# A fused cross-attention and feed-forward block: another order for the first units, feed-forward factors in five portions, and the value factor ahead of the third chunk's rows

## The chip, the cores and the metric

The kernel runs on one core of a Trainium2 chip. The metric is the device time of one execution in microseconds (us); lower is better. A core has four compute engines with queues of their own, TensorE (PE, matmuls), VectorE (DVE), ScalarE (ACT) and GpSimd (POOL), and SyncE (SP), which here issues nearly all DMAs. Each engine takes its instructions in the order of its own program; between engines there are only semaphores, waited for by hand.

## The reference, cut to what matters

```python
def reference(x, ctx, mask, g_xattn, g_ffn, ...):      # x (2, 2048, 512), ctx (2, 128, 512)
    # cross-attention, 16 heads of 32; x normalised twice, ctx once
    q = (layer_norm(_layernorm(x), g_x, b_x) @ w_q)     # 2048 queries a batch
    k, v = layer_norm(ctx, g_kv, b_kv) @ w_kv           # 128 keys a batch
    attn = softmax(where(mask == 0, -1e9, q @ k.T * SCALE))
    x = x + tanh(g_xattn[0]) * ((attn @ v) @ w_proj + b_proj)
    # feed-forward, 512 -> 2048 -> 512, weights (q - 128) * scale by groups of 128 rows
    h = layer_norm(_layernorm(x), ln_gamma, ln_beta)
    z = silu(h @ w1 + fc1_bias) @ w2 + fc2_bias
    return x + tanh(g_ffn[0]) * (_layernorm(x) + 0.5 * z)
```

(`_layernorm` is without gain and shift; the residual of the feed-forward part is its own normalised input.)

## The kernel before

All large products are made of parts: each operand is split into a high and a low part, and three matmuls (high x high, high x low, low x high) stand for one product (`split_product`).

**Attention.** The 4096 rows are 8 chunks of 512; a chunk has 4 blocks of 128 columns, that is 4 heads each. One chunk and one block make a *unit*, v = 0 to 31. Every engine has its own `step(i, k)`, and `every_step` runs it for v = 8i + k: steps -8 to 7 written out (i = 0), two rounds of a loop of 8 steps, and the last steps written out. A dictionary gives work that is put ahead of a given step (`setup`). `real(i, k, n)` tells whether the unit exists. What belongs to one unit is spread over many steps. TensorE in step k does, in this order:

- `scores_for_max(k+1)` on token tiles 0 and 1: unmasked scores, whose maximum over the keys VectorE takes (`take_max`); `ps_max` has two banks, so tile t waits for the maximum of tile t-2, and tile 1 also for `max_row` of the unit before, whose turned maxima lie in the same bank;
- the first half of `queries(k+2)`, six matmuls; then tiles 2 and 3 of `scores_for_max(k+1)`; then the second half of `queries(k+2)`, six matmuls;
- `turn_x(k+6)`: four transposes of the normalised x;
- `weighted_values(k-1)`: probabilities times values, and the sums of the probabilities; its last matmul raises `pv_done`;
- `turn_maxima(k+1)`: the maxima turned into rows;
- `scores(k, j)` for heads j = 0, 1, then (from step 5 on with halves of `project(k-5)` between) 2 and 3. There are two banks `ps_s`, so scores j wait for the exponentials of scores j-2. Scores 0 also wait for the packed queries and packed maxima, which come by DMA (`q_packed`, `max_packed`).

ScalarE in step k: `take_queries(k+2)` (`q_hi`), `take_x(k+6)` (`xt_hi`, `xt_f`), `take_maxima(k+1)` (`max_row`), then for each of four heads `p_f` and `p_hi` (`probabilities`), then `outputs_hi(k-1)` (`o_hi`). In `probabilities`:

```python
after(act, s_done, HG * v + j + 1)
after(act, *lo_taken(i, k - 1, j))
nc.scalar.activation(p_f[j][:, :], ps_s[j % 2][:, :], ACT.Exp, ...)
after(act, pv_done, v)          # weighted_values of unit v - 1 has read the old p_hi
nc.scalar.activation(p_hi[j][:, :], ps_s[j % 2][:, :], ACT.Exp, ...)
```

VectorE in step k: the maxima of unit k+1 (tiles 0, 1), `add_residual(k-6)`, maxima of tiles 2, 3, `rows_in_step(k, 0)`, `queries_lo(k+2)` (`q_lo`, waits for `q_hi`), `rows_in_step(k, 1)`, `invert_sums(k-1)` (`den_t`, `inv_t`, `inv_den`; waits for `pv_done`), `p_lo` of heads 0 and 1, `normalise(k-1)` (`o_f`). `rows_in_step` spreads the layer norm of later chunks: statistics (`row_stats`) in steps with k mod 4 = 3, `normalise_rows` in the two steps behind them; the factors between (`row_scales`, seven small operations) are GpSimd's. Chunk 2 is the third; it has its statistics in step -1 and its normalisation in steps 0 and 1.

GpSimd in step k: `xt_lo` of block k+6, the bias on the residual, `row_scales`, `p_lo` of heads 2 and 3, `o_lo(k-1)`.

SyncE in step k: `pack_queries(k+1)` (three DMAs of 256 KB, `q_dram` to `q_pack`), loads of x, residual loads and stores of the result, `store_queries(k+2)` (`q_hi`, `q_lo` to memory), `pack_maxima(k+1)` (four DMAs of 2 KB, `max_row` to `q_pack`, L491).

**Setup around the first steps.** Ahead of VectorE's step 0 stands `value_parts`: from the bound of the values it makes the scale `v_scale`, then the low part of the values (the high part is ScalarE's, `values_first_part`), and copies the four largest magnitudes `most`. Ahead of its step 6 stands `ffn_numbers`: 13 small operations that make the scales of the feed-forward part (`ffn_scales`).

**Feed-forward.** 128 steps of 24 matmuls of 512 columns, in which TensorE hardly ever waits.

Of the kernel before, what the change touches and what calls it, by code (L numbers as in the profile page):

```python
# [37 lines left out]
HG = P // HEAD  # L38
# [3 lines left out]
V_RANGE = 16384.0  # L42
W_RANGE = 0.125
H_RANGE = 356.0
Y_RANGE = 32768.0
Y_BOUND = 131072.0
# [197 lines left out]
def attention(nc, env):  # L244
# [33 lines left out]
    with ExitStack() as scope:  # L278
# [121 lines left out]
        def normal_rows(i, c):  # L400

            return x_rows(c) if real(i, KB * c, UNITS) else x_norm

        def in_tail(i, k):

            return isinstance(i, int) and PER * i + k >= UNITS - 3
# [140 lines left out]
        def _(pe):  # L547
# [96 lines left out]
            def step(i, k):  # L644
# [7 lines left out]
                if real(i, k + 1, UNITS):  # L652
                    scores_for_max(i, k + 1, (2, 3))
                if real(i, k + 2, UNITS):
                    queries(i, k + 2, second)
# [4 lines left out]
                if real(i, k + 1, UNITS):  # L660
                    turn_maxima(i, k + 1)
                if real(i, k, UNITS):
                    scores(i, k, 0)
                    scores(i, k, 1)
# [80 lines left out]
        def _(act):  # L745
# [44 lines left out]

            def step(i, k):
                if real(i, k + 2, UNITS):
                    take_queries(i, k + 2)
                if real(i, k + AHEAD, UNITS + KB):
                    take_x(i, k + AHEAD)
                if real(i, k + 1, UNITS):
                    take_maxima(i, k + 1)
                if real(i, k, UNITS):
                    for j in range(HG):
                        probabilities(i, k, j)  # L800
                if real(i, k - 1, UNITS):
                    outputs_hi(i, k - 1)
                if isinstance(i, int):
                    last_steps(PER * i + k)
# [59 lines left out]
        def _(dve):  # L864
# [78 lines left out]
            def rows_in_step(i, k, half):  # L943

                c = k // KB + 2
                spread = not isinstance(i, int) or 2 * i + c >= 2 and real(i, KB * c, UNITS)
                if k % KB == 3 and (not isinstance(i, int) or 2 * i + c + 1 >= 2):
                    row_stats(i, c + 1, range(TT // 2 * half, TT // 2 * (half + 1)))
# [7 lines left out]
            def step(i, k):  # L956
# [9 lines left out]
                if real(i, k + 2, UNITS):  # L966
                    queries_lo(i, k + 2)
                rows_in_step(i, k, 1)
                if real(i, k - 1, UNITS):
# [63 lines left out]

            def ffn_numbers():

# [4 lines left out]
                nc.vector.tensor_scalar(w2_scale, inv_most[:, 2:3], W_RANGE, None, ALU.mult)  # L1040
                nc.vector.tensor_scalar(h_gain, lng_c, inv_most[:, 0:1], H_RANGE, ALU.mult, ALU.mult)
                nc.vector.tensor_scalar(h_shift, lnb_c, inv_most[:, 0:1], H_RANGE, ALU.mult, ALU.mult)
                link(nc.vector.tensor_tensor(y_unscale, most[:, 0:1], most[:, 1:2], ALU.mult))
                link(nc.vector.scalar_tensor_tensor(out=y_bound, in0=y_unscale, scalar=Y_BOUND, in1=most[:, 3:4],
                                                    op0=ALU.mult, op1=ALU.add))
                link(nc.vector.tensor_scalar(y_unscale, y_unscale, 1.0 / (W_RANGE * H_RANGE), None, ALU.mult))
                link(nc.vector.reciprocal(y_scale, y_bound))
                link(nc.vector.tensor_scalar(y_scale, y_scale, Y_RANGE, None, ALU.mult))
                link(nc.vector.tensor_tensor(z_unscale, y_bound, most[:, 2:3], ALU.mult))
                dve.wait_ge(tanh_ready, 2)  # L1050
                nc.vector.tensor_scalar(z_unscale, z_unscale, half_gate[:, :], 1.0 / (W_RANGE * Y_RANGE),
                                        ALU.mult, ALU.mult).then_inc(scales_ready, 1)

# [37 lines left out]

            def value_parts():

                dve.wait_ge(v_summed, 1)
                link(nc.vector.reciprocal(v_bound[:, :], ps_s[0][:, 0:1]))
                link(nc.vector.tensor_scalar(scale16[:, :], all_ones[:, 0:HEAD], v_bound[:, :], V_RANGE, ALU.mult, ALU.mult))
                nc.vector.tensor_copy(v_scale[:, :], scale16[:, 0:1]).then_inc(v_scaled, 1)
                dve.wait_ge(v_scaled, 1)
                for b in range(B):
# [3 lines left out]
                last.then_inc(v_ready, 1)  # L1103
                dve.wait_ge(most_spread, 1)
                nc.vector.tensor_copy(most, ps_s[1][:, 0:4]).then_inc(most_ready, 1)
                nc.vector.memset(pause[:, :], 0.0).then_inc(setup_over, 1)

            def last_steps(u):

                if u in (UNITS + 1, UNITS + 3):  # L1110
# [3 lines left out]
            every_step(dve, step, {-8: context_rows, -7: lambda: [masks(), scale_maxima()], -4: lambda: [key_parts(), row_stats(0, 1), key_means()], -1: lambda: [value_bound(), scale_maximum()],  # L1114
                              0: value_parts, 6: ffn_numbers})

        @block.gpsimd
        def _(pool):
# [64 lines left out]
            def step(i, k):  # L1183
# [4 lines left out]
                if k == FIRST:  # L1188
                    row_scales(i, 0)
                if k % KB == 3 and (not isinstance(i, int) or 2 * i + k // KB + 3 >= 2):  # L1190
                    row_scales(i, k // KB + 3)
# [3 lines left out]
                if real(i, k - 1, UNITS):  # L1195
                    outputs_lo(i, k - 1)
                if isinstance(i, int) and PER * i + k == UNITS:
                    sum_scales()
# [372 lines left out]
```

## Time and profile before

| what | value |
|---|---|
| median of 3 runs | 1101.06 us (1099.99 to 1102.05) |
| the profiled execution, its own time | 1101.9 us |
| its span, first to last instruction | 1100.1 us |
| mean granted TensorE clock | 0.981 of full |
| TensorE busy | 1034.4 us, 94% |
| VectorE, ScalarE, GpSimd busy | 648.1, 399.2, 328.7 us |
| attention steps 0 to 7 | 52.3 to 147.3 us |
| feed-forward part | from about 415 us to the end |

The profiled execution's time is 0.8 us above the median, its span 1.0 below it. Engines overlap, so busy times don't add up; what matters is where TensorE stands still.

### The profile page before, as it was taken

The numbers are of one execution on the slowest core, as the hardware profiler recorded it, in microseconds if no ns is written. First come the engines' busy times: TensorE is split into PE (matmuls) and PEld (weight loads), VectorE is DVE, ScalarE is ACT, GpSimd is POOL, SyncE is SP. The second block draws the span as 40 slices with busy tenths as digits, with TensorE's granted clock in tenths as the row PEclk, the third lists the DMA queues.
The fourth block names the chain that finished last, engine by engine and source line by source line (L and its number), as shares of the span: only waits on it lengthen the run. The fifth ranks groups of instructions, "written<-read, shape, count | busy, mean of one in ns | idle before, by whom it ended". The sixth has DMA issues, their size and how long they took to land.

```text
span 1100.1 us, 15132 instructions
## 1 busy us (share of the span) xinstructions
PE 1034.4 (94%) x5182; PEld 564.0 (51%) x5182; DVE 648.1 (59%) x1070; ACT 399.2 (36%) x612; POOL 328.7 (30%) x338
## 2 busy tenths in 40 slices
PE   5777899999999878999999999999999999999998
PEld 3444567767766553444444444444444444444443
DVE  5667798898888757786335335346345335335322
ACT  3457577777776633331121121121121121121111
POOL 4545477677675442202102102102102012012000
PEclk9889899999999989999999999999999999999999
DMA  8566567778666669602001001100100200200101
GB/s 275 134 163 175 163 192 212 213 201 238 194 196 179 188 185 278 239 1 77 1 1 49 28 1 39 39 1 28 51 1 1 77 1 1 77 1 1 39 1 39
DMA packets 61473, 109.38 MB, mean 99 GB/s; under 512 B 9656, under 2 KB 10848, under 8 KB 60896
## 3 DMA queue, kind: packets, MB, share of 16 engines
q1 hardware_dynamic: 58632, 104.11, 31.2%
q10 hardware_dynamic: 2776, 4.40, 1.4%
q8 instruction: 41, 0.67, 0.3%
q14 instruction: 24, 0.20, 0.1%
HBM read 72.57 MB, written 33.55 MB: 96 GB/s over the span
## 4 chain that ended last, share of the span: by engine, by line
PE 57%; DVE 3%; issue 1%; ACT 1%; DVEq 0%
PE ps_z L1387 9%; PE ps_z L1389 9%; PE ps_z L1388 9%; PE ps_y L238 9%; PE ps_y L240 9%; PE ps_y L239 9%; PE ps_h L1401 1%; DVE w_f L192 1%; ACT w_hi L183 1%; DVE w_lo L195 0%; DVE y_hi L1448 0%; DVE x_in L1509 0%; DVE x_stats L1489 0%; DVE x L1471 0%; DVE x_norm L1501 0%
## 5 line engine op out<-in xcount | busy, mean ns | idle before, releaser
L1422 ACT ACTIVATE y_f<-ps_y,cols,ffn_scales 128x512 f32<-128x512 f32 x128 | 99.4, 777 | 489.5 <-PE ps_y L240 489.5
L1448 DVE TENSOR_SCALAR y_hi<-y_f,ffn_scales 128x512 f16<-128x512 f32 x128 | 70.0, 547 | 330.4 <-ACT y_f L1422 330.4
L1387 PE MATMUL ps_z<-w_hi,y_hi 128*128 128x512 f16 x512 | 194.7, 380 | 3.6 <-DVE w_lo L195 3.6
L238 PE MATMUL ps_y<-ht_hi,w_hi 128*128 128x512 f16 x512 | 194.1, 379 | 1.6 <-PEq L278 1.5
L1388 PE MATMUL ps_z<-w_lo,y_hi 128*128 128x512 f16 x512 | 194.6, 380 | 0.0
L1389 PE MATMUL ps_z<-w_hi,y_lo 128*128 128x512 f16 x512 | 194.6, 380 | 0.0
L239 PE MATMUL ps_y<-ht_lo,w_hi 128*128 128x512 f16 x512 | 194.0, 379 | 0.0
L240 PE MATMUL ps_y<-ht_hi,w_lo 128*128 128x512 f16 x512 | 194.0, 379 | 0.0
L1450 DVE SCALAR_TENSOR_TENSOR y_lo<-y_f,ffn_scales,y_hi 128x512 f16<-128x512 f32 x128 | 103.2, 806 | 4.6
L761 ACT ACTIVATE p_f<-ps_s,fill_col 128x512 f32<-128x512 f32 x128 | 86.2, 673 | 3.5 <-PE ps_s L592 3.5
L763 ACT ACTIVATE p_hi<-ps_s,fill_col 128x512 f16<-128x512 f32 x128 | 85.3, 666 | 0.0
L870 DVE TENSOR_REDUCE maxima<-ps_max 128x4 f32<-128x512 f32 x128 | 81.9, 680 | 5.6 <-PE ps_max L569 5.3
L238 PEld LDWEIGHTS ps_y<-ht_hi,w_hi 128*128 128x128 f16 x512 | 50.1, 98 | 62.6 <-issue 2.5
L1152 POOL TENSOR_TENSOR p_lo<-p_f,p_hi 128x512 f16<-128x512 f32 x58 | 67.8, 1175 | 47.9 <-ACT p_hi L763 47.5
L1387 PEld LDWEIGHTS ps_z<-w_hi,y_hi 128*128 128x128 f16 x512 | 50.2, 98 | 61.3 <-DVE w_lo L195 4.1
L1389 PEld LDWEIGHTS ps_z<-w_hi,y_lo 128*128 128x128 f16 x512 | 50.2, 98 | 60.9 <-issue 0.8
L240 PEld LDWEIGHTS ps_y<-ht_hi,w_lo 128*128 128x128 f16 x512 | 50.1, 98 | 60.4
L239 PEld LDWEIGHTS ps_y<-ht_lo,w_hi 128*128 128x128 f16 x512 | 50.1, 98 | 60.2
L1388 PEld LDWEIGHTS ps_z<-w_lo,y_hi 128*128 128x128 f16 x512 | 50.2, 98 | 57.6 <-issue 0.6
L1527 POOL TENSOR_TENSOR ln_a<-x_mean_var,eps 128x4 f32<-128x4 f32 x7 | 1.6, 224 | 254.9 <-DVE x_mean_var L1494 254.9
L1545 POOL TENSOR_TENSOR x<-x,b_rows 128x512 f32<-128x512 f32 x16 | 25.8, 1645 | 141.5 <-DVE x L1509 141.5
L907 DVE TENSOR_TENSOR p_lo<-p_f,p_hi 128x512 f16<-128x512 f32 x70 | 53.6, 783 | 19.3 <-ACT p_hi L763 18.6
(200 smaller groups left out, 1585.9 us busy)
## 6 DMA issues: line engine op xcount, KB each, us to landing
q_pack<-q_dram SPq DMA_DIRECT2D x96, 256.0 KB, 4.0
q_dram<-q_hi SPq DMA_DIRECT2D x32, 256.0 KB, 3.2
q_dram<-q_lo SPq DMA_DIRECT2D x32, 256.0 KB, 3.6
x_dram<-x_out SPq DMA_DIRECT2D x32, 256.0 KB, 4.6
x_res<-in_x SPq DMA_DIRECT2D x30, 256.0 KB, 4.5
q_raw<-in_L_ffn_fc_q SPq DMA_DIRECT2D x6, 1024.0 KB, 8.8
s_raw<-in_L_ffn_fc_scales SPq DMA_DIRECT2D x6, 1024.0 KB, 11.8
x_in<-in_x SPq DMA_DIRECT2D x4, 1024.0 KB, 7.8
```

Of the source, the lines that this page charges most:

```text
L238: nc.tensor.matmul(out, s_hi, m_hi, start=(k == 0), stop=False)
L239: nc.tensor.matmul(out, s_hi, m_lo, start=False, stop=False)
L240: last = nc.tensor.matmul(out, s_lo, m_hi, start=False, stop=(k == n - 1))
L761: nc.scalar.activation(p_f[j][:, :], ps_s[j % 2][:, :], ACT.Exp, bias=fill_col[:, b:b + 1]).then_inc(p_f_ready, 1)
L763: nc.scalar.activation(p_hi[j][:, :], ps_s[j % 2][:, :], ACT.Exp, bias=fill_col[:, b:b + 1]).then_inc(p_hi_ready, 1)
L870: nc.vector.reduce_max(maxima[k % 2][:, t, :], ps_max[t % 2][:, :].rearrange("p (j n) -> p j n", j=HG), AX.X).then_inc(max_taken, 1)
L1387: nc.tensor.matmul(ps_z[t][:, :], hi, w2_hi[:, f, :], start=(f == 0), stop=False)
L1388: nc.tensor.matmul(ps_z[t][:, :], hi, w2_lo[:, f, :], start=False, stop=False)
L1389: last = nc.tensor.matmul(ps_z[t][:, :], lo, w2_hi[:, f, :], start=False, stop=(f == FB - 1))
L1422: nc.scalar.activation(y_f[f % 2][:, :], ps_y[f % 2][:, :], ACT.Silu, bias=b1_c[:, f:f + 1], scale=y_unscale).then_inc(y_f_ready, 1)
L1448: nc.vector.tensor_scalar(y_hi[f % 4][:, :], y_f[f % 2][:, :], y_scale, None, ALU.mult).then_inc(y_hi_ready, 1)
L1450: nc.vector.scalar_tensor_tensor(out=y_lo[f % 4][:, :], in0=y_f[f % 2][:, :], scalar=y_scale, in1=y_hi[f % 4][:, :], op0=ALU.mult, op1=ALU ...
```

## The change

Three things are changed.

1. For units 1 to 4 (`unprojected`: the steps that have no projection yet) TensorE issues scores 0 and 1 ahead of the second half of `queries(k+2)`, instead of behind `turn_maxima`; ScalarE does the probabilities of heads 0 and 1 first in its step, ahead of `take_queries`.
2. `value_parts` is split: `value_scale` (the scale, and the copy of `most`) stays ahead of VectorE's step 0; the low part of the values (`value_rest`) goes into step 0, behind `queries_lo`. The statistics of chunk 2 go from step -1 to step 0, behind that, its row factors on GpSimd to the end of step 0, and the normalisation of all its four tiles to step 1, behind `queries_lo`.
3. `ffn_numbers` is split into `weight_scales`, `hidden_bound`, `hidden_scales`, `row_gain` and `row_shift`, ahead of VectorE's steps 2, 3, 4, 5 and 6. `hidden_bound` has one operation more (a lower bound on `y_bound`). The ranges to which weights and hidden values are scaled, immediates of operations that were there, go from 0.125 to 2^-8 and from 32768 to 256.

```diff
-W_RANGE = 0.125
+W_RANGE = 2.0 ** -8
-Y_RANGE = 32768.0
+Y_RANGE = 256.0
...
+        def unprojected(i, k):
+            return isinstance(i, int) and 1 <= PER * i + k < 5
...
     # TensorE, step
                 if real(i, k + 1, UNITS):
                     scores_for_max(i, k + 1, (2, 3))
+                if unprojected(i, k):
+                    scores(i, k, 0)
+                    scores(i, k, 1)
                 if real(i, k + 2, UNITS):
                     queries(i, k + 2, second)
...
-                if real(i, k, UNITS):
+                if real(i, k, UNITS) and not unprojected(i, k):
                     scores(i, k, 0)
                     scores(i, k, 1)
...
     # ScalarE, step
             def step(i, k):
+                if unprojected(i, k):
+                    probabilities(i, k, 0)
+                    probabilities(i, k, 1)
                 if real(i, k + 2, UNITS):
                     take_queries(i, k + 2)
...
-                    for j in range(HG):
+                    for j in range(HG // 2 if unprojected(i, k) else 0, HG):
                         probabilities(i, k, j)
...
     # VectorE, rows_in_step
-                if k % KB == 3 and (not isinstance(i, int) or 2 * i + c + 1 >= 2):
+                if isinstance(i, int) and PER * i + k in (0, 1):
+                    if half == 1:
+                        row_stats(0, 2) if k == 0 else normalise_rows(0, 2)
+                    return
+                if k % KB == 3 and (not isinstance(i, int) or 2 * i + c + 1 > 2):
...
     # VectorE, step
                 if real(i, k + 2, UNITS):
                     queries_lo(i, k + 2)
+                if isinstance(i, int) and PER * i + k == 0:
+                    value_rest()
                 rows_in_step(i, k, 1)
...
-            def ffn_numbers():
+            def weight_scales():
                 dve.wait_ge(most_ready, 1)
                 link(nc.vector.tensor_scalar(most, most, 1e-30, None, ALU.max))
                 link(nc.vector.reciprocal(inv_most[:, 0:3], most[:, 0:3]))
                 nc.vector.tensor_scalar(w1_scale, ...)
                 nc.vector.tensor_scalar(w2_scale, ...)
-                nc.vector.tensor_scalar(h_gain, lng_c, inv_most[:, 0:1], H_RANGE, ALU.mult, ALU.mult)
-                nc.vector.tensor_scalar(h_shift, lnb_c, inv_most[:, 0:1], H_RANGE, ALU.mult, ALU.mult)
                 link(nc.vector.tensor_tensor(y_unscale, most[:, 0:1], most[:, 1:2], ALU.mult))
+            def hidden_bound():
                 link(nc.vector.scalar_tensor_tensor(out=y_bound, ...))
                 link(nc.vector.tensor_scalar(y_unscale, ...))
+                link(nc.vector.tensor_scalar(y_bound, y_bound, 1e-30, None, ALU.max))
                 link(nc.vector.reciprocal(y_scale, y_bound))
+            def hidden_scales():
                 link(nc.vector.tensor_scalar(y_scale, ...))
                 link(nc.vector.tensor_tensor(z_unscale, ...))
                 dve.wait_ge(tanh_ready, 2)
                 nc.vector.tensor_scalar(z_unscale, ...)
+            def row_gain():
+                nc.vector.tensor_scalar(h_gain, lng_c, inv_most[:, 0:1], H_RANGE, ALU.mult, ALU.mult)
+            def row_shift():
+                nc.vector.tensor_scalar(h_shift, ...).then_inc(scales_ready, 1)
...
-            def value_parts():
+            def value_scale():
                 ...
                 nc.vector.tensor_copy(v_scale[:, :], scale16[:, 0:1]).then_inc(v_scaled, 1)
+                dve.wait_ge(most_spread, 1)
+                nc.vector.tensor_copy(most, ps_s[1][:, 0:4]).then_inc(most_ready, 1)
+            def value_rest():
                 dve.wait_ge(v_scaled, 1)
                 for b in range(B):
                     dve.wait_ge(v_first, b + 1)
                     last = nc.vector.scalar_tensor_tensor(out=v_parts[1][:, b, :], ...)
                 last.then_inc(v_ready, 1)
-                dve.wait_ge(most_spread, 1)
-                nc.vector.tensor_copy(most, ps_s[1][:, 0:4]).then_inc(most_ready, 1)
                 nc.vector.memset(pause[:, :], 0.0).then_inc(setup_over, 1)
...
-                              0: value_parts, 6: ffn_numbers})
+                              0: value_scale, 2: weight_scales, 3: hidden_bound, 4: hidden_scales, 5: row_gain, 6: row_shift})
...
     # GpSimd, step
-                if k % KB == 3 and (not isinstance(i, int) or 2 * i + k // KB + 3 >= 2):
+                if k % KB == 3 and (not isinstance(i, int) or 2 * i + k // KB + 3 > 2):
                     row_scales(i, k // KB + 3)
...
                     outputs_lo(i, k - 1)
+                if isinstance(i, int) and PER * i + k == 0:
+                    row_scales(0, 2)
```

## Rows read from the trace of the kernel before

**Rows 1.** The page, busy time, share of the span and instructions, TensorE.

```profile
PE 1034.4 (94%) x5182; PEld 564.0 (51%) x5182; DVE 648.1 (59%) x1070; ACT 399.2 (36%) x612; POOL 328.7 (30%) x338
```

**Rows 2.** Windows of steps 6 and 7: stretch, busy time per engine, clock, DMA.

```profile
120.72:137.61 16.89, 12.84 (x61) 8.53 (x60) 11.82 (x26) 7.75 (x14) 6.08 (x5) 0.80 0.58 171
137.61:147.30 9.69, 9.69 (x61) 7.02 (x60) 9.49 (x21) 7.56 (x14) 7.30 (x7) 1.00 0.62 193
```

**Rows 3.** Timeline, steps -1 and 0, VectorE and TensorE: start, duration, operation, wait.

```profile
52.60 1.29 DVE L923 BATCH_NORM_STATS2 x_stats<-x_in 128x6 f32<-128x512 f32 x2 [2.09 <-DMA x_in<-in_x]
...
59.77 1.00 PE L569 MATMUL ps_max<-k_hi,q_hi 128*128 128x512 f32 x2 [3.55 <-DVE maxima L870]
```

**Rows 4.** Timeline of TensorE, end of step 1 and the scores.

```profile
73.36 0.39 PE L240 MATMUL ps_qm<-xt_hi,wq_lo 128*128 128x512 f32 x1
73.59 0.60 PE L622 MATMUL ps_xp<-ident,x_norm 128*128 128x128 f32 x4
...
77.73 0.49 PE L592 MATMUL ps_s<-q_pack,k_pack 97*128 97x512 f32 x1 [1.35 <-ACT p_hi L763]
```

**Rows 5.** Timeline of ScalarE, step 1.

```profile
73.79 0.60 ACT L750 ACTIVATE q_hi<-ps_qm 128x512 fp32r<-128x512 f32 x1 [3.48 <-PE ps_qm L240]
...
75.95 0.58 ACT L782 CAST max_row<-ps_max 4x512 fp32r<-4x512 f32 x1 [0.22 <-PE ps_max L577]
76.43 0.67 ACT L761 ACTIVATE p_f<-ps_s,fill_col 128x512 f32<-128x512 f32 x1
77.01 0.66 ACT L763 ACTIVATE p_hi<-ps_s,fill_col 128x512 f16<-128x512 f32 x1
```

**Rows 6.** SyncE's queue, packed maxima: timeline; landing of 58.1 to 58.8, of 76.5 to 78.4.

```profile
56.39 2.95 SPq L491 DMA_DIRECT2D q_pack<-max_row  x4
...
86.14 3.70 SPq L491 DMA_DIRECT2D q_pack<-max_row  x4
...
DMA to landing us min/median/max: 2.8/2.9/3.0
...
DMA to landing us min/median/max: 1.7/1.7/1.7
```

**Rows 7.** Timeline of VectorE, steps 1 to 5.

```profile
75.48 0.71 DVE L886 STREAM_TRANSPOSE den_t<-ps_den 128x512 f32<-128x512 f32 x1
...
95.67 1.28 DVE L923 BATCH_NORM_STATS2 x_stats<-x_norm 128x6 f32<-128x512 f32 x2
...
97.38 0.68 DVE L886 STREAM_TRANSPOSE den_t<-ps_den 128x512 f32<-128x512 f32 x1
...
100.79 2.68 DVE L870 TENSOR_REDUCE maxima<-ps_max 128x4 f32<-128x512 f32 x4
104.67 0.69 DVE L877 SCALAR_TENSOR_TENSOR q_lo<-ps_qm,q_hi 128x512 fp32r<-128x512 f32 x1 [1.20 <-ACT q_hi L750]
105.28 1.00 DVE L940 TENSOR_SCALAR x_norm<-x_norm,x_mean_var,ln_r 128x512 f32<-128x512 f32 x2
106.19 0.71 DVE L886 STREAM_TRANSPOSE den_t<-ps_den 128x512 f32<-128x512 f32 x1
...
116.50 0.71 DVE L886 STREAM_TRANSPOSE den_t<-ps_den 128x512 f32<-128x512 f32 x1
```

**Rows 8.** Timeline of VectorE and TensorE, the feed-forward factors and behind them.

```profile
121.15 1.16 DVE L1037 TENSOR_SCALAR ffn_scales<-ffn_scales 128x4 f32<-128x4 f32 x1
...
123.42 1.31 DVE L1042 TENSOR_SCALAR ffn_scales<-cols,ffn_scales 128x4 f32<-128x4 f32 x1
...
126.75 1.30 PE L569 MATMUL ps_max<-k_hi,q_hi 128*128 128x512 f32 x2 [4.05 <-DVE maxima L870]
```

**Rows 9.** Timeline of GpSimd beside them.

```profile
123.44 1.26 POOL L1132 TENSOR_TENSOR o_lo<-o_f,o_hi 128x512 fp32r<-128x512 f32 x1
```

**Rows 10.** A window of 3.2 us behind the scores of step 3, columns as in rows 2.

```profile
88.40:91.60 3.20, 3.14 (x7) 2.48 (x8) 2.56 (x4) 2.80 (x6) 1.91 (x2) 0.50 0.26 55
```

More of the change, by code:

```diff
@@ L1050, in ffn_numbers @@
                 dve.wait_ge(tanh_ready, 2)
-                nc.vector.tensor_scalar(z_unscale, z_unscale, half_gate[:, :], 1.0 / (W_RANGE * Y_RANGE),
-                                        ALU.mult, ALU.mult).then_inc(scales_ready, 1)
+                nc.vector.tensor_scalar(z_unscale, z_unscale, half_gate[:, :], 1.0 / (W_RANGE * Y_RANGE), ALU.mult, ALU.mult)
+            def row_gain():
+                nc.vector.tensor_scalar(h_gain, lng_c, inv_most[:, 0:1], H_RANGE, ALU.mult, ALU.mult)
+            def row_shift():
+                nc.vector.tensor_scalar(h_shift, lnb_c, inv_most[:, 0:1], H_RANGE, ALU.mult, ALU.mult).then_inc(scales_ready, 1)
             def key_parts():
```

## The prediction

> **What bounds the kernel now.** I read the page first: TensorE is busy for 94% of the span [rows 1], so a change pays only where TensorE stands still or its clock is low. Then I cut the first 150 us into the kernel's own steps (one unit per step). From step 7 on a step takes 9.69 us, with TensorE busy in every one of them; step 6 takes 16.89 us, at a clock of 0.80 [rows 2]. Everything behind step 7 follows TensorE, so what the first steps win or lose should arrive at the end one to one. Last I read the timelines of each engine through steps 0 to 6, for which wait ends last there.
>
> I count from T(v), the moment at which `weighted_values` has finished unit v-1 in step v. VectorE's `den_t` starts at once behind it, so the trace has it: T(1) = 75.48, T(5) = 116.50, thus 41.0 us for four cycles [rows 7].
>
> Three losses are seen. In step 0 TensorE waits 3.55 us for VectorE's maxima, which stand behind the statistics of chunk 2 (these waited 2.09 us for their rows from memory) and the value factor [rows 3]. In each of steps 1 to 4 it waits 1.35 us ahead of score 2, for the exponential of head 0, and again, more shortly, ahead of score 3 [rows 4]. In step 6 it waits 4.05 us for maxima behind `ffn_numbers` [rows 8], and its matmuls are slow for a while after.
>
> **The change, part by part.**
>
> *Step 0.* With the statistics gone from step -1, `q_lo`(1), the value scale and the maxima of unit 1 come as soon as TensorE delivers them, and the 3.55 us wait goes. What is late next is the packed maximum of unit 0: SyncE issues its four small DMAs from 56.39, behind the query DMAs of its in-order queue, which the change leaves alone; the last is issued at 58.8 and lands 2.9 later [rows 6], so scores(0,0) come at 61.7, not at 64.3. The first exponential follows 0.5 later, the next three starts 0.57 apart and 0.66 for the last [rows 5]: score 3 at 64.6. Then, at 0.23 a matmul [rows 4], two scores for the maxima, six of queries, two, the two early scores of unit 1 and six more end at 69.0; turning x and the weighted values take 1.89 [rows 4, 7]: T(1) = 70.9, **4.6 us earlier**. The statistics of chunk 2 (2.4, plus 0.5 to join them) now lie behind the value factor, under the wait for those scores; GpSimd's row factors for them come behind its share of unit 0, near 68 to 71.5, before step 1's normalisation wants them.
>
> *The new order, steps 1 to 4.* TensorE now issues scores 0 and 1 of unit k ahead of the second half of queries(k+2), the turn of x and `weighted_values(k-1)`; ScalarE takes `p_f`, `p_hi` of both heads ahead of `take_queries(k+2)`. But `probabilities` waits for `pv_done` before it writes `p_hi`, and that is `weighted_values(k-1)`, which stands behind the early scores. So ScalarE starts `p_hi`(0) only at T, and queued behind it are everything that it did before T in the old order. From T, with the starts of [rows 5]: `p_hi`(0) at 0.05, `p_f`(1), `p_hi`(1), then `q_hi` at 1.76, done at 2.36; from its start to the end of the two copies of x it is 1.94 (73.79 to 75.95, less the wait of 0.22), so `max_row` runs from 3.70 to 4.28. Two chains leave here.
> VectorE has stood waiting in `queries_lo` since about T-2: `q_lo` from 2.40, `den_t` 0.61 on, from there 3.41 to the first maximum of unit k+2 (inversion, two `p_lo`, `o_f`), and 1.29 for two maxima [rows 7]: T+7.71. Only then may TensorE score tile 3, at +0.23 issue S0(k+1), S1, and with 0.23 x 6 of queries and 1.89 reach T(k+1) = T + 11.67.
> SyncE: `max_row` at 4.28, fourth DMA issued 1.8 later, landed 1.7 later [rows 6]: T+7.8. The two chains end together, so neither alone being shorter helps. The old waits ahead of scores 2 and 3 become one before tile 1 (for `max_row`, which lives in the same PSUM bank) and one before tile 2.
>
> *What VectorE gets on that chain.* Whatever stands between `q_lo` and the maxima lengthens a cycle in full. Cycle 1: all four tiles of chunk 2 normalised in one go, 1.8 (0.91 for two [rows 7]), and the first portion of the feed-forward factors, about 0.8. Cycle 2: four small dependent operations of 0.19, one of them new: 0.8. Cycle 3: the second half of the statistics of chunk 3, 1.7 [rows 7], and a portion of 0.5. Cycle 4: two tiles 0.9 and the row gain, 0.4. Sum 6.9. So 4 x 11.67 + 6.9 = 53.6 against 41.0: **12.6 us later**.
>
> *Step 6.* Of `ffn_numbers` (from 121.15; TensorE gets its maximum at 126.75) one operation is left ahead of the maxima. It is four columns wide, yet one such took 1.31 us and ended at 124.73, just as GpSimd's operation ended at 124.70 [rows 8, 9]. I give it 1.25, of which the step's slack takes 0.35, so 0.9 on TensorE; with the plain step of 9.7 to 9.8 [rows 2] that is 10.7 for 16.9: **6.2 us earlier**. Three of the old operations were of the long kind; spread out they cost 0.15 where GpSimd is idle, 1.2 where it is not. That is the bound of each portion; I take the short value except in steps 5 and 6.
> The Trainium skill ("SBUF — State Buffer", Who interferes with whom) says that VectorE and GpSimd share a pair of SBUF ports as an exclusive lock and that a tensor_scalar can take it; the ends in rows 8 and 9 agree. By that rule the normalisation of cycle 1, itself a tensor_scalar, could also stand behind GpSimd's `xt_lo` of 1.3 us, which would make the sum about 1.2 larger.
>
> *The clock.* TensorE runs at 1.2 instead of 2.4 GHz in some stretches after it stood still: 3.2 us at 0.50 from 88.40 [rows 10], the matmuls then 0.43 apart instead of 0.23. In steps 1 to 4 of the old trace this hit two of four cycles, about 1.2 us each. At the start the new kernel stands still from 58.0 to 61.7 and nearly so to 64.6, so I expect the 12 matmuls up to the early scores slow: 12 x 0.2 = **2.4 us later** (bounds 0 and 4.5). In the new cycles the critical TensorE work is the tail (six queries, turn, weighted values), worth 2.6 if all slow. TensorE is now idle some 5 us or more of 12 to 14. Bounds: nothing, and 4 x 2.6 = 10.4; I take two hits of half size beyond those already in the 41.0, **2.7 us later**.
>
> *No cost.* `W_RANGE` and `Y_RANGE` are immediates of operations that stay; feed-forward matmuls, weights and DMAs are the same instructions. SyncE's program is unchanged. `value_rest` ends near 60, ahead of the exponentials at 62.2, which cover it.
>
> Sum: -4.6 + 2.4 + 12.6 + 2.7 - 6.2 = +6.9 us. The profiled execution took 1101.9 (span 1100.1), 0.8 above the median of 1101.06. On the median: **1108.0 us**.
>
> **Rivals.**
> 1. *The clock stays up in the new cycles and at the start.* For it: of four gaps of one size in the old steps only two were followed by a slow stretch. Sum 1.8: 1102.9, no measurable change. This is also the case in which the three parts merely cancel. Against it: the gaps grow.
> 2. *Faster: the early exponentials do not lengthen the cycle.* If `weighted_values` were done by the time that ScalarE wants it, and VectorE's tail lay beside TensorE's work, four cycles stay at 41.0: -4.6 + 2.4 - 6.2 = -8.4, 1092.7. It decides below 47.2 us for the four (11.8 each), where the gain reaches 0.2%. Against it: my bare cycle alone is 11.67 and the known extras add 1.7 each.
> 3. *Packed maxima later.* At 86.14 the four issues took 3.70 instead of some 2.4 us [rows 6], just after a chunk of x was fetched, hidden there; in the new order it ends the chain. Twice 2 us: 1112.
> 4. *The port lock in cycle 1 and in the portions*: 1.2 more, 1109.2; no case of its own.
>
> **How the numbers follow.** Chances: forecast 0.60, rival 1 0.13, rival 2 0.14, rival 3 0.13. 0.2% (2.2 us) is what this kernel's times can tell from none. Slower 0.73, same 0.13, faster 0.14. The forecast's own range is 1104 to 1113 (cycle clock 0 to 7 us). The range reaches down into rival 2's slow half, 1098, and up to 1113; the all-slow bound (1117) is left out.
>
> **What the profile would show.** Right: scores(0,0) near 61.7; T(1) near 73; `q_hi` of steps 1 to 4 directly behind two or more exponentials that start at T; VectorE idle 4 us before each `q_lo` there; cycles of 12.5 to 16; no 4 us wait in step 6; T(5) near 130, T(6) near 140 and some 7 later than before (116.50 + 16.9). Wrong: `p_hi`(0) not waiting for T, or cycles near 10, would refute the main term; a T(1) near 75 the start; a step 6 above 12 the last.

## The result, and the profile after

The changed kernel takes **1118.86 us** (median of three, 1118.26 to 1120.33) against 1101.06: a ratio of 1.0167 [1.0148, 1.0186]. Slower, as forecast, but by 17.8 us and not 6.9, and outside the range of 1104 to 1113.

The page of the kernel after, busy time (share of the span) and instructions of each engine, against [rows 1]:

```profile
span 1117.0 us, 15131 instructions
PE 1043.5 (93%) x5182; PEld 567.3 (51%) x5182; DVE 651.2 (58%) x1071; ACT 399.3 (36%) x612; POOL 329.8 (30%) x338
```

VectorE has one instruction more and TensorE as many as before, with 9.1 us more of busy time for the same matmuls: part of them ran slower. To place the rest I use a mark that the prediction only wrote as T: `turn_maxima` starts on TensorE directly behind `weighted_values`. Its starts in steps 1 to 6, read off TensorE's timeline (`ps_max<-ident,maxima`), and what lies between:

| | step 1 | four cycles (1 to 5) | step 5 to 6 |
|---|---|---|---|
| before | 75.31 | 41.03 | 16.91 |
| after | 72.55 | 67.71 | 10.66 |
| difference | -2.76 | +26.68 | -6.25 |

The three differences make +17.7 at the end of step 6; the spans differ by 16.9, the medians by 17.8. So the whole loss lies in four cycles of one kind. These are marks of one execution of each kernel. A kernel below that shares all code with the kernel before up to step 1's mark reaches it at 76.83 instead of 75.31, so a difference of some 1.5 us or less between two traces is no proof of a cause. The windows of the kernel after, one cycle each and then step 6, and last a tail that is read further down. Columns: stretch, its length, busy time of TensorE, weight loads, VectorE, ScalarE, GpSimd, granted clock, DMA share, GB/s.

```profile
72.55:90.50 17.95, 11.11 (x53) 6.59 (x49) 10.93 (x20) 7.68 (x13) 5.08 (x4) 0.71 0.44 134
90.50:106.92 16.42, 11.60 (x53) 7.01 (x50) 9.97 (x17) 7.68 (x13) 5.31 (x4) 0.69 0.30 81
106.92:123.51 16.59, 10.97 (x52) 6.58 (x48) 8.52 (x21) 7.68 (x13) 8.52 (x11) 0.79 0.36 97
123.51:140.26 16.75, 10.43 (x50) 6.00 (x47) 11.03 (x17) 9.03 (x15) 5.52 (x5) 0.80 0.41 119
140.26:150.92 10.66, 10.29 (x64) 7.00 (x60) 8.42 (x13) 7.23 (x13) 5.88 (x5) 1.00 0.52 130
102.20:105.70 3.50, 3.50 (x11) 2.51 (x9) 1.38 (x3) 0.48 (x1) 0.00 (x0) 0.50 0.00 0
```

TensorE stands still for 4.8 to 6.8 us of each cycle, and the clock averages 0.69 to 0.80; in the old steps 6 and 7 it was 0.80 and 1.00 [rows 2]. No engine is busy for more than 11.6 of some 17 us: this is a chain of waits, not a busy engine. The second cycle, followed from T = 90.5, ScalarE's timeline of the kernel after (start, duration, operation, the wait ahead of it and what ended it):

```profile
90.62 0.69 ACT L770 ACTIVATE p_hi<-ps_s,fill_col 128x512 f16<-128x512 f32 x1 [3.77 <-PE ps_den L615]
91.20 0.68 ACT L768 ACTIVATE p_f<-ps_s,fill_col 128x512 f32<-128x512 f32 x1
91.77 0.69 ACT L770 ACTIVATE p_hi<-ps_s,fill_col 128x512 f16<-128x512 f32 x1
92.34 0.60 ACT L757 ACTIVATE q_hi<-ps_qm 128x512 fp32r<-128x512 f32 x1
...
94.14 0.56 ACT L789 CAST max_row<-ps_max 4x512 fp32r<-4x512 f32 x1
```

`p_hi`(0) waits 3.77 us for `ps_den`, the end of `weighted_values(1)`: the wait for `pv_done` that the prediction named (2.57, 4.36 and 4.72 in the other three). Three exponentials later comes `q_hi`, at T+1.84; `max_row` stands at T+3.64. Forecast were 1.76 and 3.70. VectorE's timeline of the same cycle, and two later lines:

```profile
92.98 0.69 DVE L887 SCALAR_TENSOR_TENSOR q_lo<-ps_qm,q_hi 128x512 fp32r<-128x512 f32 x1 [6.42 <-ACT q_hi L757]
93.59 0.70 DVE L896 STREAM_TRANSPOSE den_t<-ps_den 128x512 f32<-128x512 f32 x1
...
95.25 2.50 DVE L917 TENSOR_TENSOR p_lo<-p_f,p_hi 128x512 f16<-128x512 f32 x2
97.68 0.68 DVE L909 TENSOR_TENSOR o_f<-ps_o,inv_den 128x512 f32<-128x512 f32 x1
98.28 0.50 DVE L1060 SCALAR_TENSOR_TENSOR ffn_scales<-ffn_scales 128x1 f32<-128x1 f32 x1
...
99.39 1.29 DVE L880 TENSOR_REDUCE maxima<-ps_max 128x4 f32<-128x512 f32 x2
...
129.19 3.09 DVE L917 TENSOR_TENSOR p_lo<-p_f,p_hi 128x512 f16<-128x512 f32 x2
...
145.08 1.16 DVE L1076 TENSOR_SCALAR ffn_scales<-cols,ffn_scales 128x4 f32<-128x4 f32 x1
```

VectorE stands still for 6.42 us, since its queue is held at `q_lo`; `den_t`, which it could have done at T, comes 3.1 late. And TensorE, same kernel, same cycle, with the tail up to T = 106.9:

```profile
100.23 1.30 PE L573 MATMUL ps_max<-k_hi,q_hi 128*128 128x512 f32 x2 [2.55 <-DVE maxima L880]
101.33 1.06 PE L596 MATMUL ps_s<-q_pack,k_pack 97*128 97x512 f32 x2
102.18 0.63 PE L238 MATMUL ps_qm<-xt_hi,wq_hi 128*128 128x512 f32 x1
102.61 0.63 PE L239 MATMUL ps_qm<-xt_lo,wq_hi 128*128 128x512 f32 x1
...
104.74 1.06 PE L626 MATMUL ps_xp<-ident,x_in 128*128 128x128 f32 x4
```

The last wait to end ahead of the tail is for VectorE's maxima, not for a DMA. Then the matmuls start 0.43 apart instead of 0.23 [rows 4]: the last window above has the clock at 0.50 throughout.

### The profile page after: what moved, and what is told of

Read it like the earlier page. It is cut to its first block, busy times and chain, and to the rows that moved or that the text cites. A ratio compares the mean times of both kernels' runs of the same rounds, so it can differ in the third digit from the quotient of the medians.

```text
span 1117.0 us, 15131 instructions
## 1 busy us (share of the span) xinstructions
PE 1043.5 (93%) x5182; PEld 567.3 (51%) x5182; DVE 651.2 (58%) x1071; ACT 399.3 (36%) x612; POOL 329.8 (30%) x338
## 4 chain that ended last, share of the span: by engine, by line
PE 56%; DVE 3%; issue 1%; ACT 1%; DVEq 0%
PE ps_z L1418 9%; PE ps_z L1417 9%; PE ps_z L1416 9%; PE ps_y L240 9%; PE ps_y L238 9%; PE ps_y L239 9%; PE ps_h L1430 1%; DVE w_f L192 1%; ACT w_hi L183 1%; DVE w_lo L195 0%; DVE y_hi L1477 0%; DVE x_in L1538 0%; DVE x_stats L1518 0%; DVE x L1500 0%; DVE x_norm L1530 0%
## 5 line engine op out<-in xcount | busy, mean ns | idle before, releaser
L573 PE MATMUL ps_max<-k_hi,q_hi 128*128 128x512 f32 x128 | 46.8, 437 | 26.4 <-DVE maxima L880 20.9
L1167 POOL TENSOR_TENSOR xt_lo<-xt_f,xt_hi 128x512 fp32r<-128x512 f32 x32 | 41.6, 1301 | 88.3 <-ACT xt_f L782 80.4
```

## The experiments

Two things were to be told apart: that ScalarE's early `p_hi` makes the loss, and what its excess over the forecast consists of. All times below are medians; each ratio is to the kernel before, run on the same chip, with its 95% interval. The chips differ (the kernel before had medians of 1101.6 to 1103.1 on them), so times of different experiments are best compared by their ratios. "Cycles" and "step 6" are the two columns of the table above (before: 41.03 and 16.91).

**The order taken back alone.** All else stays as in the kernel after.

```diff
-                if unprojected(i, k):
-                    scores(i, k, 0)
-                    scores(i, k, 1)
...
-                if unprojected(i, k):
-                    probabilities(i, k, 0)
-                    probabilities(i, k, 1)
...
-                    for j in range(HG // 2 if unprojected(i, k) else 0, HG):
+                    for j in range(HG):
```

> The changed kernel with the order of the first units put back on TensorE and ScalarE; the value factor, chunk 2's rows and the five portions stay as changed. Theory A (the new order of units 1 to 4 is the whole loss; the two other parts gain): the start stays about 3 to 4.6 us early, step 6 stays at 10.7 instead of 16.9 us, the four cycles go back to about 41 to 43 us instead of 67.8. Time 1090 to 1094 us. Rival B (the rows of chunk 2 and the portions on VectorE carry the loss, whatever the order): the cycles stay above 55 us, time above 1105 us.

Measured 1099.88, 0.9978 [0.9952, 1.0004]; cycles 46.95, step 6 10.67. Some 19 us of the loss are gone (21 by the ratios), so the order is its main cause. But the expectation (41 to 43, 1090 to 1094) was missed: the two other parts bring no gain that is clear of the noise, and the cycles did not go back to 41. TensorE now waits for VectorE's maxima in each of them. Its timeline in this kernel:

```profile
81.08 1.00 PE L573 MATMUL ps_max<-k_hi,q_hi 128*128 128x512 f32 x2 [1.37 <-DVE maxima L874]
...
92.43 1.01 PE L573 MATMUL ps_max<-k_hi,q_hi 128*128 128x512 f32 x2 [1.52 <-DVE maxima L874]
...
104.97 1.01 PE L573 MATMUL ps_max<-k_hi,q_hi 128*128 128x512 f32 x2 [1.12 <-DVE maxima L874]
...
115.65 1.00 PE L573 MATMUL ps_max<-k_hi,q_hi 128*128 128x512 f32 x2 [0.83 <-DVE maxima L874]
```

**The order alone**, put into the kernel before: the two edits of the change to TensorE's and ScalarE's step, with `unprojected`, and nothing else.

> The kernel before with nothing but the new order of units 1 to 4 on TensorE and ScalarE. Theory A: each cycle has the exponential that waits for the weighted values, and costs 15 to 16 us: 60 to 64 us for four instead of 41, no gain at the start or in step 6. Time 1119 to 1126 us, slower than the full change. Rival B: within 4 us of the kernel before, 1101 to 1105 us.

Measured 1122.05, 1.0167 [1.01, 1.0235]; cycles 58.43, step 6 16.85. The time came where expected, the cycles 1.6 below it: the order alone adds 17.4 us in the cycles. Expected too was that it would be slower than the full change; by the ratios the two are alike.

**ScalarE's part taken back alone**: TensorE keeps its early scores, `probabilities` stands behind `take_maxima` again.

> The changed kernel, TensorE still issuing scores 0 and 1 early, but ScalarE in the old order (queries, x and the maxima ahead of all four exponentials). Theory A (the loss is ScalarE's wait for the weighted values ahead of its copy of the queries): cycles about 41 to 43 us as in the old order, time 1090 to 1095 us. Rival C (TensorE's early scores themselves cost, because they wait for the packed maxima): cycles of 13 us or more, time above 1105 us.

Measured 1101.66, 0.9986 [0.996, 1.0013]; cycles 49.49. The total missed the expectation, but 18.2 of the 26.7 us come back with this edit alone. The cycles are 49.49 - 46.95 = 2.5 longer than with both orders taken back; 2.0 of that are slow matmuls behind TensorE's waits, and the intervals of the two ratios overlap, so a cost of the early scores by themselves is not shown.

**A second pair of `p_hi`.** The early exponentials stay; only what they wait for goes: heads 0 and 1 of units 1 and 3 write `p_hi` to other memory.

```diff
+        p_hi_odd = [all_ones[:, 256:512].bitcast(F16), g("ffn_scales")[:, 256:512].bitcast(F16)] + p_hi_even[HG // 2:]
...
-                after(act, pv_done, v)
+                after(act, pv_done, v - 1 if j < HG // 2 and unprojected(i, k) else v)
```

> The changed kernel with its order kept, but p_hi of heads 0 and 1 of units 1 and 3 written to two buffers of their own, so that the exponentials of a unit wait for the weighted values of the unit before the last only. Theory A: q_hi follows the queries at once, cycles fall to 8.5 to 10.3 us, time 1082 to 1091 us. Rival C (even without that wait the early scores wait for the packed maxima and TensorE's clock stays low): cycles of 12 us or more, time above 1100 us.

Measured 1102.49, 0.9995 [0.9968, 1.0021]; cycles 50.11. Taking the wait away gives back 17.6 us of the cycles, about as much as taking the place of the exponentials back (18.2), which shows that it is the wait and not the place. Yet the expectation (8.5 to 10.3 a cycle, 1082 to 1091) was missed: time and cycles, 12.5 on average, are those of its rival, and nothing is gained over the old order. VectorE's and TensorE's timelines in this kernel's second cycle, one after the other, say why:

```profile
88.79 0.72 DVE L902 STREAM_TRANSPOSE den_t<-ps_den 128x512 f32<-128x512 f32 x1 [0.97 <-PE ps_den L621]
...
91.64 0.68 DVE L915 TENSOR_TENSOR o_f<-ps_o,inv_den 128x512 f32<-128x512 f32 x1
...
93.36 2.87 DVE L886 TENSOR_REDUCE maxima<-ps_max 128x4 f32<-128x512 f32 x4
```

```profile
94.19 1.30 PE L578 MATMUL ps_max<-k_hi,q_hi 128*128 128x512 f32 x2 [2.32 <-DVE maxima L886]
```

Inversion, two `p_lo`, `o_f`, a portion of factors and the maxima follow T without a gap, and TensorE waits for them: VectorE is the next bound, not the packed maxima of the rival. The rival's other half, a low clock, is there: from the start of score tile 2 to the mark the four cycles take 6.91, 5.92, 4.42 and 5.38 us, where 4.41 (3.94 in the last, which has no early scores) is the length at the full clock. That is 5.4 us in all.

**GpSimd kept apart**: in the four steps GpSimd starts its low parts only when VectorE's are done, and its `xt_lo` of cycle 1 behind the normalisation.

```diff
+                if isinstance(i, int) and PER * i + k == KB + 3:
+                    pool.wait_ge(norm_ready, 3 * TT)
...
+                if unprojected(i, k) and j == 2:
+                    pool.wait_ge(o_f_ready, v)
```

> The changed kernel; GpSimd's p_lo of units 1 to 4 and its xt_lo of block 7 wait until VectorE has finished o_f and the normalisation of chunk 2, so that the two engines no longer work on SBUF at once there. Theory D (VectorE's long operations, 3.85 us for four normalised tiles, 2.50 and 3.09 for two p_lo, are waits for GpSimd): the four tiles take 1.9, each pair of p_lo 1.25; the four cycles fall by about 5 us, time 1112 to 1115 us. Rival: the long durations stay, time 1117 to 1120 us or later still by the new wait.

Measured 1113.22, 1.0108 [1.0074, 1.0142], as expected; cycles 59.56, 8.2 less than after where 5 were expected. VectorE and GpSimd of the kernel after in cycle 1 and in cycle 4:

```profile
75.64 3.85 DVE L950 TENSOR_SCALAR x_in<-x_in,x_mean_var,ln_r 128x512 f32<-128x512 f32 x4
```

```profile
76.42 1.35 POOL L1167 TENSOR_TENSOR xt_lo<-xt_f,xt_hi 128x512 fp32r<-128x512 f32 x1 [4.58 <-ACT xt_f L782]
78.05 2.46 POOL L1179 TENSOR_TENSOR p_lo<-p_f,p_hi 128x512 f16<-128x512 f32 x2 [0.28 <-ACT p_hi L770]
...
129.01 2.72 POOL L1179 TENSOR_TENSOR p_lo<-p_f,p_hi 128x512 f16<-128x512 f32 x2 [0.27 <-ACT p_hi L770]
```

and VectorE in this experiment:

```profile
76.36 1.90 DVE L950 TENSOR_SCALAR x_in<-x_in,x_mean_var,ln_r 128x512 f32<-128x512 f32 x4
...
124.60 1.25 DVE L917 TENSOR_TENSOR p_lo<-p_f,p_hi 128x512 f16<-128x512 f32 x2
```

The same four normalisations take 1.90 alone and 3.85 beside GpSimd, two `p_lo` 1.25 alone in cycle 4 and 3.09 beside it. In cycle 2 the pair took 1.53 here for 2.50. So (3.85 - 1.90) + (2.50 - 1.53) + (3.09 - 1.25) = 4.8 us went from the path directly. The other 3.4 of the 8.2 are TensorE's clock, but for small operations that nearly cancel: its gaps ahead of score tile 2 are 1.15, 0.92, 2.76 and 2.20 us here for 4.07, 2.55, 3.35 and 4.03, and from there to the mark it takes 5.79, 4.41, 6.96 and 5.50 for 6.10, 6.69, 7.05 and 6.51, together 3.7 less. So part of what VectorE loses costs twice, by itself and by the slow matmuls behind the longer gap.

**TensorE kept busy.** The gap ahead of score tile 2 is filled with repeats of a matmul already there (tile 1 of `scores_for_max`), and tile 1 itself moves from ahead of the first half of the queries to behind it; the output stays the same.

```diff
+                again = {2: 9, 3: 5, 4: 7, 5: 8}.get(k, 0) if isinstance(i, int) and i == 0 else 0
...
-                    scores_for_max(i, k + 1, (0, 1))
+                    scores_for_max(i, k + 1, (0,) if again else (0, 1))
...
+                if again:
+                    scores_for_max(i, k + 1, (1,), again)
```

> The changed kernel; in steps 2 to 5 TensorE fills its wait ahead of tile 2 with 5 to 9 repeats of the tile 1 matmul (same operands, same bank, the result unchanged). Theory E (some 9 us of the loss are slow matmuls behind these gaps, clock at 0.50): with the gaps filled the second half of the queries, the turn and the weighted values run at 0.23 a matmul, the cycles fall by 6 to 9 us, time 1109 to 1113 us. Rival: the clock is not what the gaps cost, and the repeats only add: 1119 to 1123 us.

Measured 1117.56, 1.0136 [1.0105, 1.0166]; cycles 65.69. A miss, 4.6 us above the 1109 to 1113 expected. TensorE's timeline in this kernel, cycle 2:

```profile
94.45 1.30 PE L574 MATMUL ps_max<-k_hi,q_hi 128*128 128x512 f32 x5
...
99.44 1.01 PE L576 MATMUL ps_max<-k_hi,q_hi 128*128 128x512 f32 x2 [3.47 <-DVE maxima L886]
```

Five repeats filled only 1.3 us and left a gap of 3.47, and the tail behind was slow for the most part; in cycle 1 nine repeats took 3.48 and the tail ran 0.23 apart. So the run did not do what it was for in three of four cycles, and it was made again with 9, 20, 20 and 15 repeats:

> As the kernel with TensorE's gap filled, but 9, 20, 20 and 15 repeats in steps 2 to 5 instead of 9, 5, 7 and 8, enough for the gap at 0.23 a matmul. There the first cycle, in which the repeats reached the end of the gap, had its tail at full clock and was 1.5 us shorter; in the second the repeats ended 3.5 us before the gap did and the tail was slow again. Theory E (the clock follows the gap): now all four tails run at 0.23, cycles 2 to 4 fall by some 1.7 to 2.5 us each, time 1111 to 1114 us. Rival: the tails stay slow, 1117 us or more.

Measured 1113.13, 1.0086 [1.0055, 1.0118], as expected; cycles 60.60, 7.1 less than after. The third cycle of this kernel, as a window (columns as above) and as TensorE's timeline:

```profile
103.92:118.34 14.42, 12.68 (x73) 8.54 (x70) 8.61 (x21) 7.69 (x13) 8.54 (x11) 1.00 0.43 111
```

```profile
108.71 4.71 PE L574 MATMUL ps_max<-k_hi,q_hi 128*128 128x512 f32 x20
114.42 0.50 PE L576 MATMUL ps_max<-k_hi,q_hi 128*128 128x512 f32 x1 [0.50 <-DVE maxima L886]
...
115.23 0.40 PE L238 MATMUL ps_qm<-xt_hi,wq_hi 128*128 128x512 f32 x1
...
116.62 0.60 PE L629 MATMUL ps_xp<-ident,x_in 128*128 128x128 f32 x4
```

Extra work on TensorE makes the kernel faster. In all four cycles the matmuls behind the gap now start 0.23 apart; in this one the clock is 1.00 throughout, and the cycle of 16.59 becomes 14.42. The other three average 0.88 to 0.89, since matmuls ahead of the gap and the first repeats are still slow there: they take 15.76 for 17.95, 16.02 for 16.42 (the twenty repeats start slow and hold tile 2 up by some 1.5 us) and 14.40 for 16.75.

**The portions and the rows, each alone.** The five portions of factors with their new ranges in the kernel before, at the places of the change:

> The kernel before with the five portions alone (and the ranges). Theory F: step 6 falls from 16.9 to about 10.7 us (6.2 gained), the portions in steps 2 to 5 give back 2 to 4 us, as VectorE's maxima end last there: 1098 to 1101 us against 1103 of the kernel before. Rival: the portions are free, 1096 to 1097 us.

Measured 1101.67, 0.9991 [0.9972, 1.0011]; cycles 46.46, step 6 10.67. The portions gain 6.2 us in step 6 and lose 5.4 in the cycles, where 2 to 4 were expected; the time is just above the 1098 to 1101 expected. (Step 1's mark is 1.5 later than before though nothing differs ahead of it.) Then value factor and chunk 2's rows alone, with all five portions together ahead of step 6:

> The kernel before with the second part of the change alone: value factor ahead of chunk 2's rows, the portions together ahead of step 6. Expected: the start gains 2.7 to 3 us, the four tiles normalised at once cost 1 to 2 us in the first cycle, step 6 stays near 16.9 us: 1.5 us faster than the kernel before, 1099 to 1100.5 us on its median of 1101. Rival (the start's gain is given back in full): same as before.

Measured 1100.67 (1099 to 1100.5 were expected), 0.9966 [0.9941, 0.9991]; step 1's mark at 72.90, cycles 42.09, step 6 16.97: 2.4 gained and 1.1 given back in single traces, with a gain of the whole, 0.3% by the ratio, that is barely clear of none.

**The portions behind the maxima of their step.** The old order, with each portion put behind `rows_in_step(i, k, 0)`, ahead of `q_lo`, where VectorE waits anyway (in steps 1, 2, 4, 5 and 6):

```diff
+        FACTORS = {1: weight_scales, 2: hidden_bound, 4: hidden_scales, 5: row_gain, 6: row_shift}
...
                 rows_in_step(i, k, 0)
+                if isinstance(i, int) and PER * i + k in FACTORS:
+                    FACTORS[PER * i + k]()
```

> The order of the kernel before, the start of the changed one, and the five portions moved from ahead of a step's maxima to ahead of q_lo, where VectorE waits for ScalarE anyway (steps 1, 2, 4, 5 and 6). Theory F (ahead of the maxima VectorE is the engine that ends last once a step has anything added, ahead of q_lo it waits 0.5 to 1.7 us): the waits for maxima of 1.4, 1.5, 1.1 and 0.8 us shrink by 0.5 to 1 each, time 3 to 5 us under the kernel with the old order and the portions as changed, 1095 to 1097 where that has 1100. Rival: where they stand is all one, 1099 to 1101 us.

Measured **1092.6**, 0.9922 [0.9898, 0.9947], faster than both kernels and than the 1095 to 1097 expected; cycles 41.72, step 6 9.76, step 1's mark 72.39. One window of this kernel, its second cycle, and all that is left of TensorE's waits for maxima:

```profile
84.18:93.77 9.59, 7.57 (x52) 4.73 (x49) 8.24 (x14) 7.58 (x14) 4.83 (x4) 1.00 0.50 140
```

```profile
80.23 1.00 PE L573 MATMUL ps_max<-k_hi,q_hi 128*128 128x512 f32 x2 [0.55 <-DVE maxima L874]
```

The waits of 1.37, 1.52, 1.12 and 0.83 are down to one of 0.55. What a portion takes there, 0.14 to 0.52 us an operation, comes mostly out of time in which VectorE would have waited. **Both together**, second pair of `p_hi` and portions moved:

> The new order with the two buffers for p_hi, and the portions moved ahead of q_lo: the new order with both of its handicaps gone. Theory G (VectorE's own work from the weighted values to the next maxima, 3.4 + 1.3 us, and TensorE's 3.9 behind it are 9.0 us a cycle before rows and port waits, so the old waits of TensorE ahead of scores 2 and 3 hid VectorE and were no free time): four cycles of 43 to 46 us, not under the 41.7 of the old order with the portions moved; 1094 to 1098 us. Rival (the order is sound once the wait is gone): cycles under 38 us, time under 1090 us.

Measured 1097.43, 0.9939 [0.9916, 0.9962], the time as expected; cycles 48.61 (43 to 46 were expected), not under 41.7. The early order does not beat the old one even without its wait and without the portions in the way; whether it is slower is not shown, since the two intervals overlap and this trace is of an execution of 1102.8, the slowest of the six. In it the stretches from score tile 2 to the mark take 6.88, 4.43, 5.99 and 6.59 us, 6.7 more than at the full clock: without them the cycles would be 41.9, by this estimate as long as those of the old order with the portions moved.

## Why the prediction was right in sign and too small

**The start.** Forecast T(1) 4.6 earlier less 2.4 of clock, -2.2; measured -2.76. scores(0,0) came at 61.47 for 61.7, behind the DMA of the packed maxima as the step says. Right, within what two traces can tell.

**The bare cycle.** Right in every part that can be seen: `p_hi`(0) at T+0.1, `q_hi` 1.84 for 1.76, `max_row` 3.64 for 3.70, `q_lo` 2.48 for 2.40, and the undoing runs: with ScalarE's order taken back, 18.2 of 26.7 us return, with the second buffer 17.6. With the order alone, where no portion and only one tile of chunk 2 lies in the way, four cycles were 58.4. The 46.7 of the bare ones, less 0.5 for the last, which has no early scores behind it, 0.5 of chunk 2's tile, 1.7 of chunk 3's statistics and 0.9 of its normalisation make 49.3; of the 9.1 beyond, 4.1 are three pairs of `p_lo` beside GpSimd (2.22, 2.50 and 3.10 for 1.25) and 4.7 slow tails (6.24, 5.69 and 5.53 us for 4.41, the last without early scores for 3.94), the two terms that follow.

**GpSimd's share of what VectorE gets: mis-sized.** The prediction priced it at nothing, with 1.2 for the normalisation as a bound. It was 5.4: the normalisation 3.85 for 1.8, the pairs of `p_lo` 2.50 and 3.09 for some 1.2, the first small operation 0.50 for 0.15 (2.0 + 1.3 + 1.8 + 0.35). What failed is the step "from there 3.41 to the first maximum", and with it the 1.8 for four tiles: they carried over rows in which VectorE's pair of `p_lo` (99.02, 1.25 us) had only GpSimd's small row factors of 0.20 to 0.55 us beside it. In the new order the exponentials of all four heads come in one block, and VectorE's `p_lo` run beside GpSimd's `xt_lo` and `p_lo` in cycles 2 and 4; in cycles 1 and 3 they came later and took 1.25.

**The cycle clock: mis-sized.** The step that failed is the term for slow matmuls in the new cycles. Forecast 2.7, "two hits of half size beyond those already in the 41.0". The last words are a slip in the sum: the 53.6 is built of pieces at the full clock, so the old hits of 1.2 each are not in it, and by its own words the term should have been 2.4 larger, about 5. From the start of score tile 2 to the mark the four cycles took 6.10 (84.40 to 90.50), 6.69, 7.05 and 6.51 us. At the full clock it is 4.41, as the third cycle of the order-alone kernel shows on TensorE:

```profile
114.05 1.00 PE L573 MATMUL ps_max<-k_hi,q_hi 128*128 128x512 f32 x2 [1.46 <-DVE maxima L880]
...
118.46 0.60 PE L581 MATMUL ps_max<-ident,maxima 128*4 128x128 f32 x4
```

The last cycle has no early scores behind it, so 2 x 0.23 less, 3.94. That makes 1.7 + 2.3 + 2.6 + 2.6 = 9.2. Keeping TensorE busy gave 7.1 back, with all four tails fast and some 1.5 lost to the late repeats of the second cycle. The bound of 10.4 held it; the value chosen did not, for it went by the two hits in four of the old steps, whose waits were 1.35 us, when those of the new order are 2.5 to 4.1.

The two make up the account: 53.6 + 5.4 + 9.2 = 68.2, less the 0.5 for the early scores that the last cycle does not have, against 67.7 measured. They are not independent: part of the clock's 9.2 goes when GpSimd is kept apart. In place of +6.9 the sum is -2.8 + 26.7 - 6.2 = +17.7.

**Step 6.** Forecast 10.7 and 6.2 earlier; measured 10.66 and 6.25, with the four-column operation at 1.16 for 1.25. Right. But the portions alone gave nothing, since they lose in the cycles what step 6 gains; the prediction counted that loss (2.5 for the portions) as part of the new order's chain and so did not see that it is there in the old order too.

**Rivals.** The clock staying up (1) and the faster one (2) fell with cycles of 16 to 18 us: the point of decision of (2) was 47.2 for the four. Packed maxima later (3) fell: the last of step 2's four DMAs was issued at 96.8 and lands 1.7 later, T+8.0 for T+7.8, and the waits ahead of the tail end on VectorE's maxima. The port lock (4) was true, and larger than priced: 5.4 for 1.2.

**The parts** do not simply add: order +17.4 in the cycles, portions +5.4, rows +1.1, 23.9 in sum and 26.7 together. The remaining 2.8 were not separated, and each of the three is a difference of two single traces.

## What to carry to other kernels

When work is moved up on an in-order engine, look for what each moved instruction waits for: if that is the end of something that now stands behind it elsewhere, everything queued behind it is late by the whole wait, and a second buffer only uncovers the next engine. Small operations cost next to nothing where their engine already waits (the portions moved) and more than their own length ahead of what another engine waits for (the portions alone). Price a chain anew with both neighbours at work and with TensorE's clock as its new gaps will have it; rows of a calm stretch are only the least that each can cost.

## What the runs showed of the hardware

- Two engines in SBUF at once: the fp32 tensor_scalar over four tiles of 128x512 took 3.85 us beside GpSimd's operations and 1.90 with them kept away. The Trainium skill ("SBUF — State Buffer", Who interferes with whom) says the two share a pair of ports under an exclusive lock; the trace agrees: the price, 1.95 us, is of the size of the GpSimd operations beside it (1.35 for one, 2.46 for two). That each wait is for one whole GpSimd operation is not shown.
- A one-column operation, 0.15 us in most rows, can be late too. In the kernel with the order taken back the first operation of `hidden_bound`, which has two tensor inputs, took 1.15 us beside a pair of `p_lo` of GpSimd that ran from 89.81 for 2.29; the one with a single tensor input behind it took 0.15 while that pair was still running:

```profile
89.84 1.15 DVE L1054 SCALAR_TENSOR_TENSOR ffn_scales<-ffn_scales 128x1 f32<-128x1 f32 x1
91.02 0.15 DVE L1056 TENSOR_SCALAR ffn_scales<-ffn_scales 128x1 f32<-128x1 f32 x1
```

- In the kernel after, the granted clock was 0.50 behind each gap of 2.5 to 4 us on TensorE, although it was busy for 10.4 to 11.6 of 17 us; filling the gaps with matmuls that nobody needs made the kernel 5.7 us faster (1118.86 to 1113.13; by ratios 1.0167 to 1.0086, some 9). At gaps near 1.3 us, as in the old steps, it fell in some and not in others, and one gap of 2.96 us, in the third cycle with the second pair of `p_hi`, had matmuls at the full clock behind it (4.42 us to the mark). No run settled which gaps do it.

```profile
106.27 1.01 PE L578 MATMUL ps_max<-k_hi,q_hi 128*128 128x512 f32 x2 [2.96 <-DVE maxima L886]
```
